# Letting expert row loads and result loads start earlier, and eight instead of six batches summed on TensorE

## The reference, cut to what matters

```python
logits = flat @ router_w.T
scores = jnp.sqrt(jax.nn.softplus(logits))
_, idx = jax.lax.top_k(scores + expert_bias, K)          # K = 4, 32 experts
topv = jnp.take_along_axis(scores, idx, axis=1)
topv = topv / (topv.sum(axis=-1, keepdims=True) + 1e-20)
...
def body(acc, xs):
    wg, wu, wd, p = xs
    return (acc + p[:, None] * _clamped_swiglu(flat, wg, wu, wd), None)
out, _ = jax.lax.scan(body, jnp.zeros_like(flat), (gate_w, up_w, down_w, probs.T))
out = out + _clamped_swiglu(flat, shared_gate_w, shared_up_w, shared_down_w)
...
x = x + out
```

## Time and profile before

| | |
|---|---|
| time, median of 3 runs | 691.42 us (689.58 to 693.4) |
| the profiled execution's own time | 689.39 us |
| its span, first to last instruction | 687.6 us |
| PE busy | 592.0 us (86%) |
| DVE busy | 442.0 us (64%) |
| mean granted TensorE clock | 0.965 |

### The profile page before, as it was taken

One profiled execution on the slowest core, in us unless ns is written; L12 is line 12 of the kernel. 1 busy time (PEld: TensorE's weight loads), 2 busy tenths in 40 slices (PEclk: granted clock), 3 DMA queues, 4 the chain that ended last, 5 costly groups with the idle time before them and its releaser, 6 DMA issues.

```text
span 687.6 us, 14458 instructions
## 1 busy us (share of the span) xinstructions
PE 592.0 (86%) x4117; PEld 476.3 (69%) x4117; DVE 442.0 (64%) x1374; ACT 391.8 (57%) x1156; POOL 373.1 (54%) x527
## 2 busy tenths in 40 slices
PE   0588899999998899998899778785887999999985
PEld 0488777787776688777686556553666887788863
DVE  1546656777666876757756586276655777655576
ACT  1002366766777655784657886662534666677660
POOL 6837847457455565586735434614154555555560
PEclk9999999999999999999999999896789999999999
DMA  7989999999999996123323965876443555555599
GB/s 261 263 210 335 335 334 334 332 330 324 318 311 324 317 304 209 52 59 113 118 71 110 347 208 156 275 266 211 147 125 108 163 157 162 149 164 161 158 349 345
DMA packets 130204, 155.02 MB, mean 225 GB/s; under 512 B 15216, under 2 KB 117744, under 8 KB 129744
## 3 DMA queue, kind: packets, MB, share of 16 engines
q1 hardware_dynamic: 112000, 122.50, 59.0%
q0 software_dynamic: 7632, 20.98, 8.5%
q10 hardware_dynamic: 10496, 10.62, 4.9%
HBM read 53.92 MB, written 100.28 MB: 224 GB/s over the span
## 4 chain that ended last, share of the span: by engine, by line
PE 62%; DVE 13%; POOL 7%; ACT 7%; issue 6%; DMA 3%; another core or an unknown queue 1%; SPq 1%; ACTq 0%; DVEq 0%; POOLq 0%
PE ps L416 11%; PE pc L679 11%; PE pS L383 6%; PE pS L659 4%; POOL arena L1441 4%; PE ps L461 3%; PE ps L645 2%; PE po L630 2%; PE ps L488 2%; PE ps L522 2%; PE po L406 2%; PE ps L514 2%; PE ps L505 2%; PE ps L591 2%; DMA arena<-y_rows 2%
## 5 line engine op out<-in xcount | busy, mean ns | idle before, releaser
L679 PE MATMUL pc<-arena,tk 128*128 128x128 f32 x768 | 109.5, 296 | 13.3 <-POOL arena L1441 7.2
L679 PEld LDWEIGHTS pc<-arena,tk 128*128 128x128 f32 x768 | 97.7, 203 | 25.5 <-issue 13.3
L416 PE MATMUL ps<-arena,work 128*128 x380 | 102.2, 393 | 1.4 <-ACT work L1193 1.4
L1441 POOL TENSOR_TENSOR arena<-arena 128x512 f32<-128x512 f32 x64 | 90.2, 1423 | 21.8 <-ACT arena L1239 21.6
L1455 POOL DMA_INDIRECT expert_rows<-stage,ixl x64 | 63.6, 994 | 37.0 <-DVE ixl L1056 19.4
L1306 ACT ACTIVATE work<-pS,work 128x128 f32<-128x128 f32 x256 | 72.5, 369 | 4.4 <-DVE work L958 4.0
L416 PEld LDWEIGHTS ps<-arena,work 128*128 128x128 f32 x380 | 67.5, 198 | 7.5 <-issue 1.8
L755 DVE TENSOR_SCALAR work<-ps 128x256 f32<-128x256 f32 x95 | 40.1, 422 | 46.5 <-PE ps L416 44.7
L383 PE MATMUL pS<-arena,tk 128*128 x190 | 61.1, 404 | 8.1 <-ACT tk L1188 6.5
L1183 ACT ACTIVATE tk<-work 128x128 f32<-128x128 f32 x95 | 29.4, 310 | 57.7 <-DVE work L755 48.6
L958 DVE TENSOR_REDUCE work<-pS 128x4 f32<-128x512 f32 x64 | 43.9, 685 | 24.6 <-PE pS L659 21.3
(11 more groups left out here) (317 smaller groups left out, 1463.8 us busy)
## 6 DMA issues: line engine op xcount, KB each, us to landing
expert_rows<-stage SPq DMA_DIRECT2D x32, 2080.0 KB, 20.7
work<-expert_rows SPq DMA_DIRECT2D x95, 130.0 KB
arena<-in_w SPq DMA_DIRECT2D x16, 768.0 KB
stage<-xn_rows SPq DMA_DIRECT2D x64, 130.0 KB
xn_rows<-xnD ACTq DMA_DIRECT2D x16, 512.0 KB, 4.9
arena<-y_rows SPq DMA_DIRECT2D x8, 512.0 KB, 9.9
tk<-in_tk SPq DMA_DIRECT2D x1, 2048.0 KB, 10.0
work<-y_rows SPq DMA_DIRECT2D x4, 512.0 KB
```

Source lines behind the costliest of these rows:

```text
L416: i = pe.matmul(p[U * k:U * k + U, 0:256], xgT[n % 3][:, 128 * c + U * k:128 * c + U * k + U], arena[:, 256 * c:][:, bass.ds(e, 256)], sta ...
L679: i = pe.matmul(pv, tk[:, h, 128 * d:128 * d + 128], kvv[:, ci, :, :].rearrange("p b (i h j) -> p (b i) h j", i=8, h=8)[:, :, hl, :], star ...
L1441: pool.tensor_tensor(kv[kk % 4][:, c, half, :].rearrange("p (i h j) -> p i h j", h=8, i=8), i0, i1, ALU.mult).then_inc(s_kv, 1)
```

## The change

Three edits.

1. VectorE copies the place numbers of a tile from column 256 to a new column 257 of the same buffer, after it has waited until the scatter of tile n-12 (which reads column 257) has landed. The scatter now reads column 257. A row load brings columns 0 to 256 only and waits for this copy of tile n-12 (`s_ix`) instead of the landing.
2. Loads into `arena` wait by a bound on how many tiles may still need the experts that lie there (`gone`): 66 tiles in place of 73 for k = 2 and 80 in place of 95 for k = 1. The place `far` begins at column 4864 in place of 6400. The loads of k = 1 have semaphores of their own.
3. Eight batches in place of six are summed on TensorE, eight in place of ten on VectorE. The two added banks are `ybanks`, which tiles use, so TensorE waits for the last ScalarE copy (`s_y` at 95) before its first product of the sum.

```diff
-ENDV, ENDP = (0, 1, 2, 4, 5, 6, 8, 9, 12, 13), (3, 7, 10, 11, 14, 15)
+ENDV, ENDP = (0, 1, 4, 5, 8, 9, 12, 13), (2, 3, 6, 7, 10, 11, 14, 15)
...
-        far = [arena[:, 6400 + 4096 * k:10496 + 4096 * k].rearrange("p (b d) -> p b d", d=256) for k in range(2)]
+        FAR = 4864
+        far = [arena[:, FAR + 4096 * k:FAR + 4096 + 4096 * k].rearrange("p (b d) -> p b d", d=256) for k in range(2)]
...
-        diag = [*spent, *(arena[:, 2304 + 128 * n:2432 + 128 * n] for n in range(2 * NPS))]
-        GONE3 = EARLY + 3 * NB
+        diag = [*spent, *(arena[:, 2304 + 128 * n:2432 + 128 * n] for n in range(KT * NPS - len(spent)))]
+        gone = [EARLY + (NB * 128 * KT - EARLY * U + e * (U - 1)) // U for e in range(NE)]
...
-                return far[k][:, b, :], (d_g[g], 16 * (-(-(NT - g) // 4) + 1))
+                return far[k][:, b, :], (d_in[2 + g], 64)
...
             pe.wait_ge(s_hT, NT)
-            accs = [*gbanks, *xbanks, po, banks.tiles[2]]
+            pe.wait_ge(s_y, NT)
+            accs = [*gbanks, *xbanks, po, banks.tiles[2], *ybanks]
...
                                       ALU.mult).then_inc(s_m, 1)
+                    if n >= NX:
+                        dve.wait_ge(d_y[(n - NX) % 4], 16 * ((n - NX) // 4 + 1))
+                    dve.wait_ge(d_g[n % 4], 16 * (n // 4 + 1))
+                    dve.tensor_copy(xg[n % NX][:, 257:258].bitcast(I32), xg[n % NX][:, 256:257].bitcast(I32)).then_inc(s_ix, 1)
...
             def result_steps(n):
+                pool.wait_ge(s_ix, n + 1)
                 pool.wait_ge(s_y, n + 1)
                 pool.indirect_dma_start(
-                    out=Yr, out_offset=bass.IndirectOffsetOnAxis(ap=xg[n % NX][:, 256:257].bitcast(U32), axis=0),
+                    out=Yr, out_offset=bass.IndirectOffsetOnAxis(ap=xg[n % NX][:, 257:258].bitcast(U32), axis=0),
...
                     if n >= NX:
-                        sp.wait_ge(d_y[(n - NX) % 4], 16 * ((n - NX) // 4 + 1))
+                        sp.wait_ge(s_ix, n - NX + 1)
                     r = sp.snap(half[n - n0], min_val=0, max_val=NE * NB * 128 + 384)
-                    sp.dma_start(xg[n % NX], Xs[bass.ds(r, U), 0:260]).then_inc(d_g[n % 4], 16)
+                    sp.dma_start(xg[n % NX][:, 0:257], Xs[bass.ds(r, U), 0:257]).then_inc(d_g[n % 4], 16)
...
                 if k == 2:
-                    sp.wait_ge(s_yp, GONE3)
+                    sp.wait_ge(s_yp, gone[3])
...
                 if k == 1:
-                    sp.wait_ge(s_yp, NT)
+                    sp.wait_ge(s_yp, gone[-(-(FAR + 2 * 4096) // 768)])
                     continue
...
-                        sp.dma_start(far[1][:, 4 * g:4 * g + 4, :], y1[:, 4 * g:4 * g + 4, :]).then_inc(d_g[g], 16)
+                        sp.dma_start(far[1][:, 4 * g:4 * g + 4, :], y1[:, 4 * g:4 * g + 4, :]).then_inc(d_in[2 + g], 16)
```

More of the change, by code:

```diff
@@ L325, in build @@
         (s_rw, s_rwP, s_regs) = (sem(n) for n in ("s_rw", "s_rwP", "s_regs"))
-        (s_gP, s_gT, s_gup, s_c, s_t, s_m, s_h2, s_hP, s_hT, s_yp, s_y, s_dg) = (sem(n) for n in (
-            "s_gP", "s_gT", "s_gup", "s_c", "s_t", "s_m", "s_h2", "s_hP", "s_hT", "s_yp", "s_y", "s_dg"))
+        (s_gP, s_gT, s_gup, s_c, s_t, s_m, s_h2, s_hP, s_hT, s_yp, s_y, s_dg, s_ix) = (sem(n) for n in (
+            "s_gP", "s_gT", "s_gup", "s_c", "s_t", "s_m", "s_h2", "s_hP", "s_hT", "s_yp", "s_y", "s_dg", "s_ix"))
         banks = Banks([ctx.enter_context(nc.psum_tensor(f"ps{i}", [128, 512], F32)) for i in range(4)], (d_id, 16))
```

## The result

The changed kernel takes 696.34 us (median of 8 runs, 694.53 to 702.34), the kernel before 689.64 us on the same chip (8 runs, 683.19 to 693.4). The ratio, which compares the means, is 1.0115, 95% interval 1.0071 to 1.016: slower by 7.9 us (the medians lie 6.7 us apart). Forecast were 692.5 us, 1.1 over before, and no measurable change, so the forecast was wrong.

The account below looks back on a forecast made before the run. TensorE was taken to bound the tile loop, and late result loads the end. T 668.8 + 0.5 + 8.6 + 0.8 + 7.3 + 2.7 = 688.7 against 687.6: +1.1, so 692.5 us; range 686.5 to 696.5.

Parts of the forecast that it names:

- the copies in the loop: VectorE, one copy per tile: hidden in idle time of the steady loop, cost nothing; 0.5 us in the first ticks.
- The rival of the first ticks: Copies and waits cost 0.2 to 0.3 us each where VectorE is the path, plus half clock: +3 us, 694.5; chance 0.08.
- the tail: Last tiles up to T: earlier result loads share DMA engines with scatters, so this end moves +1.7 us.
- T: End of ScalarE's last result copy, forecast at 668.8, set by the scatter of tile 89 landing at 668.42.
- The four-tile times: Scatters under load from tile 81: four tiles take 6.99, then 8.49 us, where the loop alone gives 6.56.
- the sum behind T: Closing sum after ScalarE's last result copy: 8.6 + 0.8 + 7.3 us, then 2.7 for the last store.
- 9.4 us to the first add: TensorE from T: 20 products at 0.43 us, 8.6 us, plus 0.8 for half clock, before VectorE's first add.
- The 7.3 us on VectorE: After waiting for TensorE: one add, three rounds of four products and two adds, and 0.07 us to finish.
- The store: The last store ends the span 2.7 us after the sum, as before.
- The row loads end and the k = 1 loads start: SyncE's queue: row loads done at about 642 instead of 650.85; k = 1 loads near 648.3 instead of 665.99.
- TensorE has no idle time for `arena<-y_rows`: Closing sum: all results landed by 670 instead of 679.2, so TensorE's wait for data after 672 goes.
- More backlog didn't put the scatters behind it: DMA engines take turns between queue rows, so a scatter is no later for twice the backlog.

Follow-up runs that it names:

- the run shown above: Edit 1 alone, with its copies, but row loads also wait for the landed scatter of tile n-12 as before; ratio 1.0066 to the kernel before.

## Why the prediction was wrong, step by step

**What failed: the copies in the loop.** "In the steady loop even 0.15 fits in the 0.49 us that VectorE idles per tile: nothing", and 0.5 us in the first ticks. The copies themselves do fit: each is 0.15 us long, and a tile stays at 1.64 us between the pauses. On 676 chips the 0.5 came out as 0.65, and the nothing as 0.4. But on 690 chips, and the result's is one, the loop loses 2.1 us in the first thirty tiles and 2.4 in tiles 30 to 78. The cause of those 4.5 us is what edit 1 adds to each tile, which the run with held row loads shows, and the pair of runs on one chip that differ by edit 1 alone (1.0108 and 1.0003). Of the 2.4, some 0.4 is there on 676 chips too, 0.85 is the half clock (1.7 us in four of eight traces), and the rest is the longer pause on tile 57. How a copy or a wait lengthens a pause is not shown. The rival of the first ticks (0.08, +3 us) had the engine right, but not that the loss goes on to tile 60.

The rows held signs that I passed over. In the earlier trace rows 70.53 of 72 us busy means 1.5 us of idle time in a stretch that I called full, and the pause on tile 56 is in it. VectorE was said to have no idle time from 494 to 505 us, but it is busy 9.13 of these 11 us, 3.65 of the last 5.

**What failed in part: the tail.** T was to come 1.7 us later relative to the tiles; it comes 2.8 us later on 690 chips (29.6 against 26.8) and 0.1 to 1.0 on 676 chips (26.7 to 27.65, against 26.6, the mean without edit 1). That early loads lengthen the tail was right: with late k = 3 loads it is back at 26.65 to 26.95 us. The four-tile times were near the mark too (7.4 and 7.8 measured, 6.99 and 8.49 forecast). But the step from there to T was wrong for the chip of the result. The forecast ended T with ScalarE waiting for the scatter of tile 89 to land. In the changed kernel the last copy waits for TensorE instead (1.28 us), and the 2.9 us that its tail is longer than before's stand almost wholly in two places: 1.4 between the result copies of tiles 86 and 87, in a pause like the one shown above, and 1.3 from the copy of tile 90 on, where the last tiles run on TensorE partly at half clock (1.22 us for L384 at 674.82, 0.97 in the earlier trace rows). On 676 chips ScalarE does wait for landed scatters under load, as the forecast has it, but the tail grows by 1.0 us at most. The long scatter of tile 91 does not count: it ends at 678.80, behind T.

**What was mis-sized: the sum behind T.** 19.4 forecast, 20.6 in the result and up to 21.2, so the gain of 1.1 us was none. 9.4 us to the first add became 9.9: the first product is 0.3 us late, and the first four (676.83 to 680.20) run almost wholly at half clock, which costs 1.65 and not 0.8 (the clock was down for 6.8 us, from 673.20 to 680.03, where the forecast had 2.6); against that only 18 products stand ahead of the first add, not 20. The 7.3 us on VectorE behind it became 8.0, with a further wait of 0.44 us for TensorE. The store took 2.7 as forecast. Moving the wait for `s_y` gives 0.9 to 1.3 back.

**What held.** The row loads end and the k = 1 loads start where the forecast put them, to 0.1 and 1.2 us. TensorE has no idle time for `arena<-y_rows`. More backlog didn't put the scatters behind it. Edit 2 without edit 3 turns the early data into time: 18.15 to 19.54 us behind T, against 20.0 to 20.6 for every kernel without edit 2 and 3.

**The sum on 690 chips**: 2.1 + 2.4 for the copies, 2.8 for the early loads in the tail, 0.3 behind T (20.63 and 21.12 in two traces of the change, 20.51 and 20.61 before): 7.6 us. Measured were 7.9 (the result, 1.0115) and 7.5 (the change in the last table, 1.0109). The first of these terms rests on means whose traces overlap. The stretch ahead of the loop is not in the sum: it scatters by 4 us (484.6 to 488.7 without copies, 485.3 to 489.3 with them), and its means differ by 1.2. So the agreement is closer than the terms deserve.

**No version beats both kernels everywhere.** Edit 2 alone gains 0.32% on a 676 chip and nothing on a 690 chip (0.9998 [0.9974, 1.0023]).

## What to carry to other kernels

A wait that costs nothing where it stands is not worth a small instruction per tile elsewhere: 95 copies of 0.15 us with their waits, each under cover, cost 4.5 us on the chips where the engines pause. Loads that are freed early can lengthen the tiles that they now run beside, here by 0 to 1 us on one kind of chip and 2.8 on the other; check what the next wait is before a load is moved ahead. Before a forecast, look through the timelines for idle time that no row explains; it was there. And a change tried on one chip can come out half as large as on another. When a part of a sum is moved to another engine, its first instruction must not wait for a bank that only a late part of it needs.

## What the runs showed of the hardware

**Chips differ in one place of a program.** The kernel before takes 676 us on two chips and 689 to 693 on the others. The expert loop's first thirty tiles take 58.9 to 59.0 us without copies on the first kind and 62.9 to 66.9 on the second, though tiles between pauses take 1.64 us on both.

**Pauses of VectorE and ScalarE together.** Some 1 to 3 us at tiles 7 to 16, 0.7 to 2.2 us at tile 56 or 57, and with early result loads again at tile 87, only on 690 chips, with nothing in the profile to hold them. Kernels without copies have the first two. The page's part 3 lists small packets of kind "instruction" on queues 8 and 14 (here of the changed kernel), 40 in place of 41 on queue 14 before:

```profile
q8 instruction: 36, 0.59, 0.3%
q14 instruction: 41, 0.34, 0.2%
```

None of them was under way in the pauses of the run shown above (the nearest start at 504.2 and 517.7, and at 587.7 and 606.5). In the pause in the tail of the changed kernel one was: an 8 KB packet of queue 14, 0.3 us long, at 662.0. Why the engines pause, why only on some chips, and how the copies lengthen it, stays open.

**A scatter that takes its engine 6 us.** GpSimd's indirect scatter is 0.96 us long, but under early result loads that of tile 91 or 92 takes 4.5 to 7.7 us, in nine of the ten traces that have such loads (not in the one with added traffic), on both kinds of chip. In the traces without them the longest takes 2.5 us. It ends behind T in all nine and cost nothing here, since the sum needs no result of these tiles. With edits 1 and 2 (T is 657.42):

```profile
655.40 7.67 POOL L1385 DMA_INDIRECT y_rows<-tk,work  x1 [1.82 <-ACT xnA L1203]
```
